# Row numbers of the gathers computed by TensorE from a five-row table of ids, and a new order for tile 1's rounding

## What is computed

```python
def _L0_cond_ref(x, condition, weights):          # weights: 16 x 32 x 32
    W = weights[condition]
    return jnp.einsum('bct,bcd->bdt', x, W)

def _L1_cond_ref(x, adapter_mapping, W, b, lora_As, lora_Bs):
    SCALING = 2
    base_out = jnp.einsum('bti,oi->bto', x, W) + b
    A = lora_As[adapter_mapping]                  # of 32: 512 x 16
    Bm = lora_Bs[adapter_mapping]                 # of 32: 16 x 512
    lora_h = jnp.einsum('bti,bir->btr', x, A)
    lora_out = jnp.einsum('btr,bro->bto', lora_h, Bm)
    return base_out + lora_out * SCALING

x = x + _L0_cond_ref(x, itok_B_0_15, L0_cond_weights)
x = x + _L1_cond_ref(x, itok_B_0_23, L1_cond_W, L1_cond_b, L1_cond_lora_As, L1_cond_lora_Bs)
```

## Time and profile before

| | |
|---|---|
| time, median of 3 runs | 85.16 us (85.14 to 85.26) |
| time of the profiled execution | 84.83 us |
| its span | 83.0 us |
| TensorE busy | 78.5 us, 94% of the span |
| VectorE busy | 60.1 us, 72% |
| ScalarE busy | 52.4 us, 63% |
| GpSimd busy | 33.5 us, 40% |
| share of the chain that ended last | TensorE 85%, DMA 6% |

### The profile page before, as it was taken

How to read it: one execution, slowest core, us unless ns; L and a number is a source line. 1 busy time by engine, 2 the same in 40 slices (tenths; PEclk the granted TensorE clock), 3 DMA queues, 4 the chain that set the end, 5 groups by cost and what they waited for, 6 DMA issues and landing times.

```text
span 83.0 us, 2012 instructions
## 1 busy us (share of the span) xinstructions
PE 78.5 (94%) x524; PEld 71.2 (86%) x524; DVE 60.1 (72%) x158; ACT 52.4 (63%) x180; POOL 33.5 (40%) x75
## 2 busy tenths in 40 slices
PE   4999599999999999999999999999999999999970
PEld 2376498899999999999999999999999999999950
DVE  2049595877879787777878787978777777869560
ACT  1555758866666675958666666667685867665520
POOL 6108843744443517080715344352608071304300
PEclk9999999999999999999999999999999999999999
DMA  2899899998476766877668778667774626130334
GB/s 24 279 349 317 202 253 216 355 252 247 142 233 197 255 197 241 198 230 196 183 205 200 210 190 241 173 238 184 236 179 155 167 91 175 30 118 0 126 126 126
DMA packets 16141, 16.07 MB, mean 193 GB/s; under 512 B 10241, under 2 KB 10626, under 8 KB 16130
## 3 DMA queue, kind: packets, MB, share of 16 engines
q1 hardware_dynamic: 14016, 11.67, 46.9%
q0 software_dynamic: 1248, 4.06, 18.6%
q10 hardware_dynamic: 866, 0.21, 1.1%
HBM read 11.74 MB, written 4.19 MB: 192 GB/s over the span
## 4 chain that ended last, share of the span: by engine, by line
PE 85%; DMA 6%; ACTq 3%; ACT 2%; DVE 1%; issue 1%; DVEq 0%
PE z_ps L565 58%; PE z_ps L602 9%; DMA a_raw<-in_lora_a 6%; PE y_ps L617 4%; PE y_ps L615 4%; PE y_ps L613 4%; PE ht_ps L589 2%; ACTq L326 1%; PE ht_ps L652 1%; PE z_ps L597 1%; DVE y_sb L552 1%; ACT L320 1%; ACTq L316 1%; ACT a_sb L391 0%; ACTq L317 0%
## 5 line engine op out<-in xcount | busy, mean ns | idle before, releaser
L565 PE MATMUL z_ps<-wa,x_hi 128*128 128x288 f32 (+2 forms) x240 | 50.1, 301 | 0.0
L565 PEld LDWEIGHTS z_ps<-wa,x_hi 128*128 128x128 f32 x240 | 38.0, 188 | 1.8 <-issue 0.5
L565 PE MATMUL z_ps<-wa,x_lo 128*128 128x288 f32 (+2 forms) x120 | 35.3, 295 | 0.0
L565 PEld LDWEIGHTS z_ps<-wa,x_lo 128*128 128x128 f32 x120 | 22.6, 188 | 0.0
L303 POOL CAST m_hi<-m_raw 128x128 fp32r<-128x128 f32 x16 | 4.8, 301 | 35.3 <-ACT m_raw L340 35.3
L294 POOL DMA_INDIRECT b_raw<-in_lora_b,b_index_slot x16 | 16.8, 1048 | 4.4 <-POOL b_index_slot L292 4.4
L384 ACT CAST z_hi<-z_ps 128x256 fp32r<-128x256 f32 x31 | 10.1, 376 | 10.2 <-PE z_ps L602 10.1
L487 DVE TENSOR_TENSOR z_lo<-z_ps,z_hi 128x256 fp32r<-128x256 f32 x31 | 11.8, 420 | 6.3 <-ACT z_hi L384 6.3
L340 ACT COPY m_raw<-w_raw 32x32 f32 x64 | 13.8, 216 | 1.8 <-DVE w_raw L519 0.9
L446 DVE TENSOR_TENSOR x_lo<-x_raw,x_hi 128x512 fp32r<-128x512 f32 x14 | 9.7, 690 | 3.7 <-ACT x_hi L352 3.7
L467 DVE TENSOR_TENSOR b_lo<-b_raw,b_hi 128x512 fp32r<-128x512 f32 x15 | 10.4, 691 | 0.5
(11 more groups left out here) (58 smaller groups left out, 76.7 us busy)
## 6 DMA issues: line engine op xcount, KB each, us to landing
out<-y_sb SPq DMA_DIRECT2D x15, 256.0 KB, 2.4
x_raw<-in_xt SPq DMA_DIRECT2D x14, 256.0 KB, 3.2
a_raw<-in_lora_a SPq DMA_DIRECT2D x60, 32.0 KB, 2.9
first_sb<-in_first SPq DMA_DIRECT2D x2, 384.0 KB, 3.9
first_sb<-in_first SPq DMA_DIRECT2D x3, 256.0 KB, 4.8
b_raw<-in_lora_b,b_index_slot POOLq DMA_INDIRECT x16, 4.0
bias_sb<-in_bias SPq DMA_DIRECT2D x1, 256.0 KB, 4.3
a_raw<-in_lora_a ACTq DMA_DIRECT2D x4, 32.0 KB
```

The costliest lines, as they stand in the source:

```text
L565: done = nc.tensor.matmul(target, (x_lo if lo_x else x_hi)[s][:, k, :], moving(lo_w), start=first and not lo_x and not lo_w, stop=last and ...
```

## The change

The host now sends a table of five rows (`ids_by_j`, 5 x 272): four rows of ids (one for each sequence of a tile) and a row of ones, beside two matrices that say which sequence a partition belongs to (times 16) and its r. VectorE turns the table into floats, and TensorE makes all row numbers by two small matmuls into PSUM, from where VectorE copies them to `b_index`. On VectorE both steps now stand ahead of `add_identity(0)`; on TensorE the two matmuls stand ahead of the seventh of now eight warm-up matmuls. On ScalarE the copy of tile 0's A comes ahead of `round_x1(0)`, and `round_a(1)` comes between the two halves of `round_x1`; VectorE's rests follow the same order.

```diff
--- before.py
+++ after.py
@@ -14,7 +14,8 @@
 ALPHA = 32
 
 
-def lora_residual_program(nc, first, xt, ids_row, ids_of_p, w0, bias, lora_a, lora_b, out):
+def lora_residual_program(nc, first, xt, ids_row, ids_by_j, w0, bias, lora_a, lora_b, out):
+
 
 
 
@@ -31,7 +32,8 @@
     B = TILES * J
     SCALING = float(ALPHA // R)
 
-    WARM_UP = (512,) * 8 + (256,)
+    WARM_UP = (512,) * 7 + (256,)
+    INDEX_AT = 6
     NX = 3
     NA = 3
     NB = 3
@@ -72,8 +74,8 @@
         scratch = sb("scratch", [P, 1], F32)
 
         ids_sb = sb("ids_sb", [1, 2 * B], I32)
-        ids_p_sb = sb("ids_p_sb", [P, TILES + 1], I32)
-        r_of_p = sb("r_of_p", [P, 1], F32)
+        ids_by_j_sb = sb("ids_by_j_sb", [J + 1, TILES + 2 * P], I32)
+        ids_by_j_f = sb("ids_by_j_f", [J + 1, TILES + 2 * P], F32)
         b_index = sb("b_index", [P, TILES], U32)
         b_index_slot = [sb(f"b_index_slot{s}", [P, 1], U32) for s in range(NB)]
 
@@ -107,7 +109,7 @@
         ht_ps = ctx.enter_context(nc.psum_tensor("ht_ps", [P, 512], F32))
 
         ids_loaded = sem("ids_loaded")
-        ids_p_loaded = sem("ids_p_loaded")
+        ids_by_j_loaded = sem("ids_by_j_loaded")
         w0_loaded = sem("w0_loaded")
         bias_loaded = sem("bias_loaded")
         first_loaded = [sem(f"first_loaded{n}") for n in range(len(PIECES) - 1)]
@@ -124,7 +126,8 @@
         mask0_step = sem("mask0_step")
         mask_ready = sem("mask_ready")
         m_zero = sem("m_zero")
-        r_ready = sem("r_ready")
+        ids_by_j_ready = sem("ids_by_j_ready")
+        b_index_computed = sem("b_index_computed")
         b_index_ready = sem("b_index_ready")
         b_index_copied = sem("b_index_copied")
         w0_plus_i = sem("w0_plus_i")
@@ -197,6 +200,8 @@
         def z_of(u, half):
             return z_ps[u % 2][:, half, Z_PS[u % 2]:Z_PS[u % 2] + HALF]
 
+        index_ps = y_last[:, 0:TILES]
+
         def y_part(n):
 
             return (y_ps[LAST % 2][:, 0:HALF], y_last[:, 0:P], ht_ps[:, 0:P])[n]
@@ -314,7 +319,7 @@
         @block.scalar
         def _(act):
             act.dma_start(ids_sb[:, :], ids_row).then_inc(ids_loaded, 16)
-            act.dma_start(ids_p_sb[:, :], ids_of_p).then_inc(ids_p_loaded, 16)
+            act.dma_start(ids_by_j_sb[:, :], ids_by_j).then_inc(ids_by_j_loaded, 16)
 
             act.wait_ge(zeros_ready, 1)
             act.copy(scratch[:, :], zeros[:, 0:1])
@@ -386,12 +391,12 @@
             round_w(0)
             round_w(1)
             round_w(2)
-            round_x1(0)
             act.wait_ge(a_loaded[0], 16 * J)
             act.copy(a0_sb[:, :, :].rearrange("p k (j r) -> p k j r", j=J),
                      a_raw[0][:, :, :, :].rearrange("p j k r -> p k j r")).then_inc(a0_ready, 1)
+            round_x1(0)
+            round_a(1)
             round_x1(1)
-            round_a(1)
             round_w(KC - 1)
             round_x(2)
             round_a(2)
@@ -494,24 +499,20 @@
                 nc.vector.tensor_tensor(y_sb[u % 2][:, :], y_ps[u % 2][:, :], bias_sb[:, :],
                                         ALU.add).then_inc(y_ready, 1)
 
-            def index_b():
-                dve.wait_ge(ids_p_loaded, 16)
-                nc.vector.tensor_copy(r_of_p[:, :], ids_p_sb[:, TILES:TILES + 1]).then_inc(r_ready, 1)
-                dve.wait_ge(r_ready, 1)
-                nc.vector.tensor_scalar(b_index[:, :], ids_p_sb[:, 0:TILES], float(R), r_of_p[:, 0:1],
-                                        ALU.mult, ALU.add).then_inc(b_index_ready, 1)
-
+            dve.wait_ge(ids_by_j_loaded, 16)
+            nc.vector.tensor_copy(ids_by_j_f[:, :], ids_by_j_sb[:, :]).then_inc(ids_by_j_ready, 1)
+            dve.wait_ge(b_index_computed, 1)
+            nc.vector.tensor_copy(b_index[:, :], index_ps).then_inc(b_index_ready, 1)
             dve.wait_ge(ident_ready, 1)
             add_identity(0)
             add_identity(1)
-            index_b()
             rest_w(0)
             for k in range(1, KC - 1):
                 add_identity(k + 1)
                 rest_w(k)
             rest_x1(0)
+            rest_a(1)
             rest_x1(1)
-            rest_a(1)
             rest_w(3)
             dve.wait_ge(mask0_step, 3)
             mask_ht(0)
@@ -554,7 +555,14 @@
         @block.tensor
         def _(pe):
             pe.wait_ge(zeros_ready, 1)
-            for columns in WARM_UP:
+            for n, columns in enumerate(WARM_UP):
+                if n == INDEX_AT:
+
+                    pe.wait_ge(ids_by_j_ready, 1)
+                    nc.tensor.matmul(index_ps[:, 1:TILES], ids_by_j_f[:, TILES:TILES + P], ids_by_j_f[:, 1:TILES],
+                                     start=True, stop=True, skip_group_check=True)
+                    nc.tensor.matmul(index_ps[:, 0:1], ids_by_j_f[:, TILES + P:], ids_by_j_f[:, 0:1],
+                                     start=True, stop=True, skip_group_check=True).then_inc(b_index_computed, 1)
                 nc.tensor.matmul(ht_ps[:, 0:columns].rearrange("p (a c) -> p a c", c=P), zeros[:, :],
                                  zeros[:, :].rearrange("p (a c) -> p a c", a=1).broadcast_to([P, columns // P, P]),
                                  start=True, stop=True)
@@ -716,15 +724,17 @@
     x0 = xt[0].reshape(P, T)
     wt = _np.asarray(inputs["L1_cond_W"]).T.reshape(KC, P, -1).transpose(1, 0, 2)
 
-    ids_of_p = _np.repeat(adapter.reshape(TILES, J).T, C, axis=0)
-    ids_of_p[:, 0] = adapter[_np.arange(P) // R % J]
+    p = _np.arange(P)
+    rows_of_b = [_np.concatenate([R * (j_of_p == _np.arange(J).reshape(J, 1)), (p % R).reshape(1, P)])
+                 for j_of_p in (p // C, p // R % J)]
+    ids_by_j = _np.concatenate([adapter.reshape(TILES, J).T, _np.ones((1, TILES), dtype=_np.int32)])
 
     laid = {
         "first": _np.concatenate([x0[:, 0:2 * P], wt[:, 0], x0[:, 2 * P:], wt[:, 1], wt[:, 2], wt[:, 3],
                                   xt[1].reshape(P, T)], axis=1),
         "xt": xt[2:],
         "ids_row": _np.concatenate([adapter, cond]).astype(_np.int32).reshape(1, 2 * B),
-        "ids_of_p": _np.concatenate([ids_of_p, (_np.arange(P) % R).reshape(P, 1)], axis=1).astype(_np.int32),
+        "ids_by_j": _np.concatenate([ids_by_j] + rows_of_b, axis=1).astype(_np.int32),
         "w0": w0.transpose(1, 0, 2),
         "bias": _np.broadcast_to(_np.asarray(inputs["L1_cond_b"]), (P, T)),
         "lora_a": lora_a.reshape(-1, KC, P, R).transpose(0, 2, 1, 3),
```

## The result

| | before | after |
|---|---|---|
| median of four runs | 85.15 us (85.08 to 85.26) | 86.34 us (86.18 to 87.72) |
| ratio | | 1.0133, 95% interval 1.0103 to 1.0163 |
| profiled execution, its span | 84.83 us, 83.0 us | 86.50 us, 84.8 us |

The changed kernel is slower by 1.3%, 1.2 us. I had said slower, but 85.44 us, and the result lies outside my range of 84.9 to 86.0. It lies where the rival that I had called *late clock* put it, at 86.4. Every ratio and its interval leave out runs more than 1.5% above a kernel's fastest, here the one of 87.72 us.

What follows compares the result with a forecast made beforehand. TensorE, busy 94%, was taken to bound the kernel; the change only shifts tile 2's start, by the later of two overlapping delays: +0.28 us on 85.16, 85.44 us. Range 84.9 to 86.0.

Steps and rivals of the forecast that it cites:

- late clock: Rival, chance 0.12: the 1.4 us hole in TensorE's warm-up delays the rise to 2.4 GHz; tile 2 at 16.24, 86.4 us.
- The step that failed: TensorE's tile 0 behind the warm-up: sixteen records at half the warm-up's 0.42 us take 3.4 us, from 6.24 to 9.65.
- a hole of 1.4 us: TensorE's warm-up: idle from 3.6 us, after six matmuls, until the index matmuls start at 5.05.
- The new order: ScalarE rounds W's last quarter 0.31 us later, so z's rest ends at 15.17, tile 2 starts at 15.31; bounds +0.2 to +0.35.
- If A lands as before: Condition on tile 0's A: ScalarE then copies it at 8.92 us and rounds W's last quarter at 10.25.
- The two delays: At tile 2's start: TensorE's work ends at 15.14, the chain through z's rest at 15.31; they do not add.
- The index steps: Ahead of tile 0: table lands 4.6 us, cast 0.35, matmuls 0.55, copy 0.23; `add_identity(0)` 1.46 late, TensorE's tile 0 at 6.24.
- My reading of the queues: ScalarE's load queue moves only 2 packets from 1.5 to 3.8 us, so the small table lands at 4.6 us.
- early table: Rival, chance 0.16: engines alternate queues, table lands about 3 us, first gather delays tile 1's A; 85.5 to 85.85 us.
- VectorE's cover: VectorE ahead of tile 1: the delay is hidden, the rest of W's third quarter ending about 9.3, before x's rest at 9.67.
- The gathers: `b_index` ready at 5.9 instead of 6.09 us gains nothing, since TensorE wants the first gather only at 12.0.

Runs made afterwards that it cites:

- e10: The kernel before with twelve dense warm-up matmuls in place of nine: 84.80 us, ratio 0.9986, none of twelve runs above 86 us.
- e7: The kernel before with four warm-up matmuls of 512 columns, so TensorE idles 1.30 us until its first data: 85.71 us, ratio 1.0081.
- g2: The kernel before with thirteen warm-up matmuls and, behind the eighth, two float32 matmuls of the index shapes on zeros: 87.24 us, five of six at 87.0 or above.
- e2: The kernel before with only the new order on ScalarE and VectorE: 85.32 us, ratio 1.0057.
- e9: The changed kernel unchanged, measured again over twelve runs: 86.16 us, eight of twelve above 86 us.
- e6: The kernel before with the five-row table, cast behind the first `add_identity`, index matmuls behind tile 0's first quarter, warm-up and order unchanged: 85.22 us, ratio 1.0037.
- f1: The changed kernel with thirteen warm-up matmuls, index matmuls behind the eighth: 86.53 us, seven of fourteen at 87.0 or above.
- f4: The changed kernel with the old order and thirteen warm-up matmuls, index matmuls behind the eighth: 85.54 us, five of twelve above 87.
- e1: The changed kernel with ten warm-up matmuls in place of eight, index matmuls behind the eighth: 86.06 us, five of ten above 86.
- e3: The changed kernel with the old order on ScalarE and VectorE, so only the index computation is new: 86.09 us, ratio 1.0102.
- e5: The changed kernel with the old order and ten warm-up matmuls, index matmuls behind the eighth: 85.24 us, ratio 1.0054, one of twelve above 86.
- f3: The kernel before with one warm-up matmul fewer, and twenty tiny matmuls before the seventh, which waits for the first data: 85.22 us, ratio 1.0027.
- e12: The kernel before with the new order, but W's last quarter rounded ahead of the second half of tile 1's x: 84.85 us, ratio 0.9986.
- g1: The kernel before with thirteen warm-up matmuls and 28 tiny bf16 matmuls behind the eighth: 87.09 us, four of six at 86.9 or above.

## Why the prediction was wrong

*The step that failed* is, in its words, "Tile 0's 16 records took 3.84 us with waits for data in them; at half of the warm-up's 0.42 they take 3.4, which I use". That took it for granted that the clock would be up by 6.24 us. The forecast itself had put a hole of 1.4 us and two small matmuls into the warm-up, and no row showed that the rise would still come in time behind them. It came at 9.35 us, and the sixteen records took 5.27 us, 1.9 more than my term. I had named this as the rival *late clock*, 86.4 us, and given it 0.12. The Trainium skill (TensorE: Matmul & The Clock Gate, Part 1) has the clock start low and be released by sustained work; the traces agree in kind: 0.427 us a record until 9 to 10 us in the changed kernel against 0.216 from tile 0's second record on, at 6.4 us, in e10. I had set it aside because no row of the kernel before has a hole. That was no reason for a small chance: no row spoke against it either, and its price was four times that of the forecast. That its 86.4 is so near the median of 86.34 is partly luck: it put tile 2 at 16.24, and the trace has 16.77.

*What the rival had wrong in its reasons.* It laid the delay to the hole alone. A hole as long as it assumed does put the rise off (e7, 1.30 us), but the changed kernel has only 0.64 us of idle time, and two small float32 matmuls without any hole are enough in 5 of 6 runs (g2). How much of the delay in the changed kernel belongs to its idle time stays open.

*The new order:* right in mechanism and nearly in size, where A lands as before. W's last quarter was to be rounded at 10.25 and is at 10.21 in e2; tile 2 was to start at 15.31 behind z's rest and starts at 15.21. That is 0.21 us in the trace; by medians it costs 0.43 (85.32 against 84.89; by the ratio's interval 0.25 to 0.7), where my bounds were 0.2 to 0.35. In the changed kernel the quarter came at 10.99 and not at 10.25, for the forecast's condition, "If A lands as before", failed: the copy of A stands at 9.67, and in e9 at 9.65. TensorE reaches tile 2 only at 16.77 us, and z's rest ends at 16.00. The two delays lie side by side, as I had said, but both are larger, and the other one ends last. By the estimate above my sum would have been too low in this execution even with the clock up in time.

*The index steps:* they were mis-sized, both ways. The table landed at 1.39 + 2.69 = 4.08 us, I had 4.6; the cast took 0.29 for my 0.35; the index matmuls 0.94 (4.45 to 5.39) for my 0.55, at the low level; the copy 0.17 for 0.23. Together tile 0 starts at 6.00, I had 6.24. My reading of the queues was half right:

```profile
q10 hardware_dynamic: 12, 0.01, 0.9%
```

This is ScalarE's queue from 1.5 to 3.8 us after the change. It moved 12 packets there and not 2, so the few packets of the small table did go out before 3.8 us. The *early table* rival had it near 3, so it was wrong too; the value lies between.

*VectorE's cover:* right. The rest of W's third quarter ends at 8.20 + 0.68 = 8.88 (I had 9.3), far ahead of x's rest. *The gathers:* right; an earlier `b_index` gains nothing (e6).

*What stays open.* I know the late clock from the spacing in one profiled execution per kernel and from times that fall in two groups. What makes one execution of a program reach the higher level at 4.6 us and the next at 10 isn't shown by these runs. Five dense matmuls behind the thin ones don't prevent it (f1, f4). Why tile 0's A landed late in both profiles of the changed kernel (copied at 9.67 and 9.65), and not in e1 (9.10), e3 (8.76) or e5 (8.98), isn't shown either; in f3, with the old table and the old order, it was as late, at 9.57. The change's two causes overlap, so that 0.4 us (order) and 1.2 (index steps alone) don't add up to the 1.2 of the whole.

No version beats the kernel before beyond the uncertainty: e10 and e12 are both at 0.9986 with intervals that hold 1.

## What to carry to other kernels

- Work put into a warm-up isn't free because TensorE has nothing to do there. Keep the warm-up dense and unbroken, and place small matmuls and waits behind it; a longer dense warm-up cost nothing here (e10), 0.9 us of thin matmuls in it cost 2 us in 21 of 38 runs (f1, f4, g1, g2).
- When a chain of waits ends at the bound engine, look for a second that ends within a tenth of it, and follow every reordering through that one too.
- A rival with a large price and no row for or against it deserves its chance by that ignorance. One profile can't show a moment that differs from run to run; look at the spread of the times.
